# Four residual graph layers with layernorm: six adjacency tiles and two of six units' sums turned in bank M1, layers and features at later steps, row maxima read over 128 partitions

## Time and profile before

| what | us |
|---|---|
| median of 3 runs | 1768.12 (1765.34 to 1771.2) |
| the profiled execution, its own time | 1762.62 |
| its span, first to last instruction | 1760.8 |
| one graph of the middle (last maximum to last maximum) | 203 |

### The profile page before, as it was taken

How to read it: one execution, slowest core, us unless ns; L and a number is a source line. 1 busy time by engine, 2 the same in 40 slices (tenths; PEclk the granted TensorE clock), 3 DMA queues, 4 the chain that set the end, 5 groups by cost and what they waited for, 6 DMA issues and landing times.

```text
span 1760.8 us, 22052 instructions
## 1 busy us (share of the span) xinstructions
PE 1454.2 (83%) x7728; PEld 718.8 (41%) x7728; DVE 1384.5 (79%) x1623; ACT 1241.6 (71%) x1475; POOL 1089.5 (62%) x581
## 2 busy tenths in 40 slices
PE   4487889898889889888889888988899987888745
PEld 3233334444444444444444443444444443344313
DVE  3567788878898778888888778987888788888654
ACT  2377878777687777777787777777687777777521
POOL 1056676676676666676576667776666766766642
PEclk9788989999899999999999999999999999999767
DMA  5413142122413133221522234130432214000000
GB/s 77 61 32 48 31 66 40 46 30 39 70 31 46 26 52 51 52 36 26 68 40 43 25 55 58 39 44 17 63 46 52 30 37 55 21 12 24 15 6 9
DMA packets 55067, 71.42 MB, mean 41 GB/s; under 512 B 21814, under 2 KB 42814, under 8 KB 54958
## 3 DMA queue, kind: packets, MB, share of 16 engines
q0 software_dynamic: 13824, 18.01, 13.7%
q1 hardware_dynamic: 41134, 52.01, 11.4%
HBM read 102.29 MB, written 3.26 MB: 60 GB/s over the span
## 4 chain that ended last, share of the span: by engine, by line
PE 45%; DVE 24%; issue 12%; ACT 11%; SPq 3%; POOL 3%; DMA 2%; ACTq 0%; POOLq 0%; DVEq 0%
PE M L586 11%; DVE RUN L823 9%; PE M L535 9%; PE Z L496 8%; PE Z L498 7%; ACT LS L677 6%; PE Z L509 4%; DVE LS L837 4%; ACT LS L685 3%; SPq L286 2%; DVE X L922 2%; POOL LS L403 2%; PE Z L596 2%; DVE RUN L820 2%; PE Z L657 2%
## 5 line engine op out<-in xcount | busy, mean ns | idle before, releaser
L403 POOL TENSOR_TENSOR LS<-LS,MB 125x1000 f32<-125x1000 f32 x384 | 894.7, 2346 | 489.4 <-DVE LS L837 334.8
L823 DVE TENSOR_TENSOR RUN<-Z,RUN 125x1000 f32<-125x1000 f32 x528 | 631.0, 1195 | 208.7 <-ACT LS L677 203.4
L677 ACT ACTIVATE LS<-Z 125x1000 f32<-125x1000 f32 x576 | 574.5, 998 | 262.0 <-PE Z L498 261.4
L685 ACT ACTIVATE LS<-LS 125x1000 f32<-125x1000 f32 x576 | 594.5, 1033 | 71.3 <-POOL LS L403 56.2
L496 PE MATMUL Z<-AT,BI 126*125 126x500 fp8e4 x1152 | 386.0, 418 | 140.1 <-DVE RUN L823 107.0
L535 PE MATMUL M<-LS,V 125*18 125x500 f32 x2304 | 326.7, 642 | 57.8 <-ACT LS L685 57.0
L498 PE MATMUL Z<-FS,FO 96*125 96x500 bf16 x1152 | 360.1, 395 | 0.0
L837 DVE TENSOR_TENSOR LS<-LS,MB 125x1000 f32<-125x1000 f32 x192 | 283.2, 1475 | 4.9 <-DMA MB<-row_maxima 2.8
L496 PEld LDWEIGHTS Z<-AT,BI 126*125 126x125 bf16 x1152 | 140.7, 146 | 282.9 <-DVE RUN L823 164.5
L498 PEld LDWEIGHTS Z<-FS,FO 96*125 96x125 bf16 x1152 | 165.5, 144 | 111.4 <-issue 21.3
L586 PE MATMUL M<-AT,XP 125*128 125x500 fp8e4 x756 | 206.8, 396 | 0.7 <-ACTq L735 0.7
(11 more groups left out here) (118 smaller groups left out, 1039.6 us busy)
## 6 DMA issues: line engine op xcount, KB each, us to landing
MB<-row_maxima SPq DMA_DIRECT2D x48, 488.3 KB
A<-in_adj_dram POOLq DMA_DIRECT2D x96, 183.1 KB, 4.8
FO<-PARTS SPq DMA_DIRECT2D x192, 46.9 KB, 2.1
FS<-PARTS SPq DMA_DIRECT2D x192, 46.9 KB, 2.1
XP<-in_x_dram SPq DMA_DIRECT2D x8, 375.0 KB
XA<-in_x_dram SPq DMA_DIRECT2D x8, 375.0 KB
out_dram<-X SPq DMA_DIRECT2D x7, 375.0 KB
row_maxima<-LMAX SPq DMA_DIRECT2D x48, 3.9 KB
```

Of the source, the lines that this page charges most:

```text
L403: nc.gpsimd.tensor_tensor(rows, rows, MB[:, u % 2, :, :], ALU.subtract).then_inc(sub_pool, 1)
L677: nc.scalar.activation(LS[:P, q % RL, :, :], banks("Z", q)[:P], ACT.Prelu, alpha=0.2).then_inc(bent, 1)
L685: nc.scalar.activation(rows, rows, ACT.Exp, scale=0.25).then_inc(exps, 1)
L823: nc.vector.tensor_tensor(run, z, run, ALU.max).then_inc(maxed, 1)
```

## The change

- `TURNS` names a bank for each tile: tiles at r = 3, 6, 8, 16, 18, 20 use the ring, those at r = 10, 14, 46, 50, 52, 64 (six; the last graph has only the first two) use M1. Before, all 12 were in the ring, at r = 3, 5, 7, 9, 11, 13, 16, 18, 45, 46, 47, 49.
- The sums of units 1 and 4 of each graph (turned at r = 48 and r = 12) use M1, the other four the ring. VectorE frees M1 after its own last read, with a wait for its own result and a semaphore instruction.
- `MEANS` is 28, 46, 64, 82, `FEATURES` begin at r = 17 (before 15), the third of `MIDDLES` is at r = 35 (before 32).
- SyncE's loads and the store at r = 11, 13, 29, 37 are at 13, 15, 31, 38. At r = 38 `spread_maxima` now comes first, since it stands ahead in the loop.
- RUN is turned in pieces of 125 neighbouring columns; LMAX is written to DRAM in single floats, by two DMAs (112 and 13 partitions); MB is read over 128 partitions, and the subtractions read 125 of them.

```diff
-for s_, steps_ in ((1, (3, 5, 7, 9)), (2, (11, 13, 16, 18)), (3, (45, 46, 47, 49))):
-    for k_, r_ in enumerate(steps_):
-        TURNS[r_] = (s_, k_)
-FEATURES = {15: ("XT", 0), 17: ("FT", 0), 19: ("FE", 0), 21: ("XT", 1), 23: ("FT", 1), 25: ("FE", 1),
-            27: ("XT", 2), 29: ("FT", 2), 31: ("FE", 2)}
-MIDDLES = {20: 0, 26: 1, 32: 2}
-MEANS = (25, 43, 61, 79)
+TURNS = {3: (1, 0, "ring"), 6: (1, 1, "ring"), 8: (1, 2, "ring"), 10: (1, 3, "M1"),
+         14: (2, 0, "M1"), 16: (2, 1, "ring"), 18: (2, 2, "ring"), 20: (2, 3, "ring"),
+         46: (3, 0, "M1"), 50: (3, 1, "M1"), 52: (3, 2, "M1"), 64: (3, 3, "M1")}
+G_IN_M1 = (1, 4)
+FEATURES = {17: ("XT", 0), 19: ("FT", 0), 21: ("FE", 0), 23: ("XT", 1), 25: ("FT", 1), 27: ("FE", 1),
+            29: ("XT", 2), 31: ("FT", 2), 33: ("FE", 2)}
+MIDDLES = {20: 0, 26: 1, 35: 2}
+MEANS = (28, 46, 64, 82)
...
-        MB = sb("MB", [P, 2, 2, C], f32)
+        MB = sb("MB", [128, 2, 2, C], f32)
...
-                sp.dma_start(spread[u % 2].rearrange("(h i c) -> i h c", i=P, c=ST),
-                             LMAX[:, u % 2, :].rearrange("p (h c) -> p h c", c=ST)).then_inc(max_out[u % 2], 16)
-                sp.wait_ge(max_out[u % 2], 16 * (u // 2 + 1))
+                for rows in (slice(0, 112), slice(112, P)):
+                    sp.dma_start(spread[u % 2].rearrange("(j i) -> i j", i=P)[rows], LMAX[rows, u % 2, :],
+                                 allow_slow_non_contiguous=True).then_inc(max_out[u % 2], 16)
+                sp.wait_ge(max_out[u % 2], 32 * (u // 2 + 1))
...
-                             spread[u % 2].partition_broadcast(P)).then_inc(mb_in[u % 2], 16)
+                             spread[u % 2].partition_broadcast(128)).then_inc(mb_in[u % 2], 16)
...
-                        last = nc.tensor.transpose(z[:P, hh, c * P:(c + 1) * P], RUN[:, u % 2, hh, c:C:ST], ID[:P, :P])
+                        last = nc.tensor.transpose(z[:P, hh, c * P:(c + 1) * P], RUN[:, u % 2, hh, c * P:(c + 1) * P], ID[:P, :P])
...
+            def free(*what):
+                if what in order:
+                    m1_free(order[what])
+                else:
+                    ring_free(place[what])
...
+                    g, k, where = slice_at(q)
+                    keep_adj(g, k, bank_of("T", g, k))
+                    if where == "M1":
+                        dve.wait_ge(at_ready, ST * g + k + 1)
+                        dve.sem_inc(m1_read, 1)
+                if sums_at(q):
+                    u, where = sums_at(q)
+                    keep(u)
+                    if where == "M1":
+                        dve.wait_ge(kept_seq, 5 * u + 5)
+                        dve.sem_inc(m1_read, 1)
```

More of the change, by code:

```diff
@@ L213, in slice_at, with sums_at @@
             g = NS * b + TURNS[r][0]
-            return (g, TURNS[r][1]) if g < NS * B else None
+            return (g, *TURNS[r][1:]) if g < NS * B else None
+        def sums_at(q):
+            u = unit_at(q, G_AT)
+            return None if u is None else (u, "M1" if u % UPG in G_IN_M1 else "ring")
         def layer_at(q, after):
@@ L263, in adj_resnorm, with bank_of @@
                 m1.append(("Y", *y_at(q)[:3]))
+            if slice_at(q):
+                g, k, where = slice_at(q)
+                (ring if where == "ring" else m1).append(("T", g, k))
+            if sums_at(q):
+                u, where = sums_at(q)
+                (ring if where == "ring" else m1).append(("G", u))
         place = {what: n for n, what in enumerate(ring)}
         order = {what: n for n, what in enumerate(m1)}
+        counted = {what: n for n, what in enumerate(what for what in m1 if what[0] not in "TG")}
         def banks(*what):
             return Z[:, place[what] % RZ, :, 0:C]
+        def bank_of(*what):
+            return M1[:, 0:C] if what in order else banks(*what)[:, 0, :]
         def link_of(b, l, n):
@@ L329, in _ @@
                     load_features(b, 1)
-                if r == 11 and b + 1 < B:
+                if r == 13 and b + 1 < B:
                     if b >= 2:
@@ L402, in subtract @@
                 rows = LS[:P, e % RL, :, :]
-                nc.gpsimd.tensor_tensor(rows, rows, MB[:, u % 2, :, :], ALU.subtract).then_inc(sub_pool, 1)
+                nc.gpsimd.tensor_tensor(rows, rows, MB[:P, u % 2, :, :], ALU.subtract).then_inc(sub_pool, 1)
             def power(b, l):
@@ L537, in weigh, with m1_free @@
                 last.then_inc(weighed, 1)
+            def m1_free(n):
+                if n:
+                    pe.wait_ge(m1_read, n)
+            def free(*what):
[3 more added lines that the diff above has]
+                    ring_free(place[what])
             def turn_sums(u):
                 pe.wait_ge(o4_ready, u + 2)
-                ring_free(place["G", u])
-                z = banks("G", u)
+                free("G", u)
+                z = bank_of("G", u)
                 for k in range(ST):
-                    last = nc.tensor.matmul(z[:P, 0, k * 2 * VC:(k + 1) * 2 * VC], O4[:, k * P:(k + 1) * P],
+                    last = nc.tensor.matmul(z[:P, k * 2 * VC:(k + 1) * 2 * VC], O4[:, k * P:(k + 1) * P],
                                             E[:, :, :].rearrange("p h o -> p (h o)"), start=True, stop=True)
@@ L640, in _ @@
                 if slice_at(q):
[L641 to L645, removed]
+                    g, k, _ = slice_at(q)
+                    free("T", g, k)
+                    turn_adj(ST * g + k, bank_of("T", g, k))
+                if sums_at(q):
+                    turn_sums(sums_at(q)[0])
             pe.wait_ge(kept_seq, 5 * NU)
@@ L700, in take_features @@
             def take_features(kind, b, c):
-                n = order[kind, b, c]
-                act.wait_ge(m1_filled, n + 1)
+                act.wait_ge(m1_filled, counted[kind, b, c] + 1)
                 if kind == "XT":
@@ L729, in take_collect @@
             def take_collect(b, l, c):
-                act.wait_ge(m1_filled, order["Y", b, l, c] + 1)
+                act.wait_ge(m1_filled, counted["Y", b, l, c] + 1)
                 if l or c:
@@ L739, in square @@
                 if l == 0 and b + 2 < B:
-                    act.wait_ge(m1_filled, order["XT", b + 2, NS - 1] + 1)
+                    act.wait_ge(m1_filled, counted["XT", b + 2, NS - 1] + 1)
                 nc.scalar.activation(SQ, Y[:, :, :], ACT.Square).then_inc(squared, 1)
```

22 lines of the change are left out of this document (7 added, 15 removed).

## The result

The changed kernel takes 1874.47 us (median of 4 runs, 1863.23 to 1879.33) against 1768.03 before: ratio 1.0592, 95% interval 1.0541 to 1.0644. It was forecast 3% faster and is 6% slower. The profiled execution took 1879.33 us, its span 1877.5.

A forecast was written before the change was run, and what follows sets the result against it. No engine alone was the bound: TensorE, VectorE and ScalarE wait for each other through a three-place ring. Gains 20 + 17 + 17 + 7 less 4 costs, 57 us off 1762.6, plus 5.5 to the median: 1711, range 1668 to 1757.

The forecast's parts named there:

- (c): Maxima's way through DRAM: read 3.1 us sooner, write 0.5 later, net 2.6; 17 us gained, bounds -20 and +43.
- (a): Transpose of the maxima on TensorE: neighbouring columns save 0.92 us a burst, 20 us gained, bounds 0 and 44.
- (b): Ring relieved by M1 at r = 12 to 14 and 48 to 50: 17 us gained, bounds 0 and 43.
- (d): Layers three steps later, features two: 7 us gained, bounds 76 us either way.
- The write is slow: Rival, chance 0.15: 1000 pieces of 4 bytes cost what the read gains, time 1728, at its bound 1748.
- Slower: Rival, chance 0.1: crowding at r = 10 to 14 and 46 to 50 costs 79 us, time 1790.
- More comes off: Rival, chance 0.2: ring's relief takes a third of graph losses, 91 us and 6 at the ends, time 1671.
- Given back: Rival, chance 0.1: VectorE holds the pace and takes all but the ends and some 10 us, time 1752.

## Why the prediction was wrong

The step that failed is the write's term in (c), twice.

**Its size.** It was taken as 0.5 us "as its time is that of a transfer of almost no bytes", bounded by 6.2; it is 6.5 (8.62 less 2.16), a little above the bound. Nearly empty was the wrong measure: with the same bytes, 250 pieces take 1.8 us, 500 take 3.8 and 1000 take 7.0. The packets' ends (1.56 us) would not have told it either; the landing came seven microseconds later.

**Its price.** This is the larger error, since even with 6.2 the prediction lost no more than 20 us. It valued 2.6 us in each of 48 units, 125 us, at 17 us, about a seventh, and used the same share for a later MB. (A third of its 34 us is 11, not 12; that changes nothing.) Towards an earlier MB that is the right order: the read alone lands MB 2.4 us sooner (write's issue to landing 6.43 in place of 8.87), 117 us, and gives 33, a quarter; on the new steps it is 137 us for 16, an eighth. Towards a later MB it is wrong: once the room before the first subtraction is used, half and then all of each microsecond reaches the end. Net, MB lands 5.0 us later than before (13.90 against 8.87). The time rose by some 104 us although (a), (b) and (d), as measured with the old write, take 51 off, so (c) cost about 155 us, where the prediction had a gain of 17 and a bound of -20. Against the same kernel with 16-byte pieces MB lands 7.4 us later, for some 190 us.

The rival *The write is slow* had the mechanism and its place, at 0.15, and its bound of 1748 carried the same two errors. The advice of the Trainium skill (DMA: Bandwidth & Descriptors, Rules for kernel authors) against one descriptor for each element, cited there, was borne out and should have had more weight than a row of a transfer of another kind.

The other steps, each by its own run:

- (a) The spacing was right (weight load 196 ns, forecast near 215; burst 1.12 us, forecast 1.1). It gave 31 us for 20, inside the bound of 44. That bursts outside TensorE's own stretches count too is the likely reason; no run parts them.
- (b) The stops at r = 13 and 49 went, as forecast, but M1 gave 8 us for 17, with intervals that overlap. The term priced stops of the kernel before, and two thirds of these went with the moved steps already; the two causes were counted as if they were apart. The stop that the new steps bring at r = 37 was not foreseen.
- (c) The read alone gave 33 us on the old steps and 16 on the new, for the 17 of the whole term. Before, the write of the maxima stood 2.2 us (median) behind ScalarE's `LMAX` at r = 38 and 1.8 at r = 2. With the new steps it is 0.03 at both, also at r = 2, where the prediction expected no change.
- (d) The moved steps gave 12 us for 7. With the old write, a graph of the middle takes 196 to 201 us with the old transpose and 193 to 196 with the new; 196 was forecast. The rival *Slower*, the crowding at r = 10 to 14 and 46 to 50, is not there: with those steps the kernel is 2% faster.
- Taken in this order, read, steps, M1, transpose, 33 + 12 + 8 + 31 = 84 us come off without the single floats (0.9532 is 83). So the rest of the change lies nearer to the rival *More comes off*, 91 and 6, than to the forecast's 57. *Given back* didn't happen.

Left open: why floats side by side land later than floats 64 bytes apart, and how the time would go if the subtractions began later than 18 steps after their tile; that wasn't tried.

## What to carry to other kernels

Count the pieces of a small transfer and look how close they lie in DRAM, not only at its bytes; and take its length from issue to landing, not from its packets. Before a latency is traded, find how much of it is hidden today, and price a loss beyond that room at nearly full, though a gain is worth a fraction. When a change has parts, take them one by one: here four lines, the read over 128 partitions, gave 33 us alone, nearly as much as all the moved steps and banks together (36), and the loss by one part hid the gains of all the others.

## What the runs showed of the hardware

- A DMA to DRAM of 1000 single floats: packets over at 1.56 us, landing reported after about 8.6 (two DMAs) or 7.0 us (one); 3.6 with each float 64 bytes from the next; 500 pieces of 8 bytes 3.8; 250 of 16 bytes 1.8.
- While 1000 neighbouring single floats are landing, another queue's packets of 1500 bytes take 1.3 to 1.7 us on average, otherwise 0.32.
- The same 4000-byte rows, 128 of them in place of 125: the last packet at 3.9 us in place of 6.3 after the issue, with 12 packets under way at a time in place of 5.
- TensorE's load of 125 x 125 float weights: 193 to 217 ns with steps of 4 or 8 bytes, 323 with steps of 16 (means).
- A second operand read with a step of 16 bytes: VectorE's subtraction from 1381 to 2549 ns, GpSimd's from 2349 to 2934 (means).
- Four writes of 3.9 KB to the same DRAM bytes, each after the landing of the last: 11.2 us, 2.2 for the first and 2.5 to 2.6 for each of the others (medians).
